# A four-layer kernel of 16 pipelined steps: the router's products one step later, beside the scores, and the queries' products between the halves of the last key unit

## The reference

```python
x = x + cross_attention(layernorm(x), ctx)      # Q = xWq+bq; K_hat = cos((ctx Wk+bk)Wr+br)
                                                # softmax(Q K_hat^T) @ (ctx Wv+bv)
x = x + sparse_attention(layernorm(x))          # top 8 earlier tokens by similarity, softmax over them,
                                                # message, gelu(mix*x + (1-mix)*msg, gain, bias) * scale
x = x + expert_mlp(layernorm(x))                # router: logits = xn @ Wr (8 experts), argmax,
                                                # p_max * (gelu(xn@W1[e]+b1[e]) @ W2[e] + b2[e])
```

## Time and profile before

| | us |
|---|---|
| median of 3 runs | 448.08 (447.14 to 448.7) |
| the profiled execution | 447.48 |
| its span, first to last instruction | 445.2 |
| PE busy | 409.2 (92%) |
| ACT busy | 257.2 (58%) |
| DVE busy | 248.7 (56%) |
| POOL busy | 236.4 (53%) |

### The profile page before, as it was taken

The page is one execution under the profiler, slowest core; times in us unless marked ns, Lnnn a source line. Parts: engine busy times, 40 slices in busy tenths (PEclk is TensorE's granted clock), DMA queues, the critical chain, the costliest instruction groups (busy, mean ns, idle before and its releaser), DMA issues.

```text
span 445.2 us, 10426 instructions
## 1 busy us (share of the span) xinstructions
PE 409.2 (92%) x3121; PEld 281.7 (63%) x3121; DVE 248.7 (56%) x808; ACT 257.2 (58%) x574; POOL 236.4 (53%) x458
## 2 busy tenths in 40 slices
PE   7858999999999999999994898699999999999991
PEld 6424454555545555455542677588999999998991
DVE  2637688788888989888984653534122212222210
ACT  0638778888988988889874646452333232424240
POOL 0733766767787887878855584642232322232210
PEclk9989999999999999999997999899999999999998
DMA  9988999797878979778965671454776656565100
GB/s 187 233 213 218 204 302 257 197 226 184 257 188 221 206 193 286 197 210 200 287 216 210 212 257 44 142 197 157 243 281 224 177 201 206 174 196 194 57 0 0
DMA packets 119449, 87.45 MB, mean 196 GB/s; under 512 B 78622, under 2 KB 109088, under 8 KB 119268
## 3 DMA queue, kind: packets, MB, share of 16 engines
q1 hardware_dynamic: 112820, 76.49, 61.1%
q0 software_dynamic: 3744, 9.46, 7.0%
q10 hardware_dynamic: 2832, 0.86, 1.1%
HBM read 79.15 MB, written 8.53 MB: 197 GB/s over the span
## 4 chain that ended last, share of the span: by engine, by line
PE 80%; issue 6%; POOL 4%; ACT 3%; DVE 3%; DMA 1%; SPq 1%; DVEq 0%; POOLq 0%; ACTq 0%
PE pK L1481 17%; PE pT L1468 17%; PE pT L1443 11%; PE pK L1443 11%; PE b L1389 5%; PE b L1626 4%; PE b L1522 4%; PE b L1586 3%; PE b L1565 3%; PE b L1615 2%; PE b L1549 1%; DMA XF<-in_ctx_dram 1%; PE pK L1389 1%; POOL f_row L408 1%; PE b L1634 1%
## 5 line engine op out<-in xcount | busy, mean ns | idle before, releaser
L1258 ACT ACTIVATE XF<-pT,b_now 128x128 f32<-128x128 f32 x184 | 52.6, 369 | 99.4 <-PE pT L1468 95.7
L1481 PE MATMUL pK<-W,XF 128*128 x368 | 86.2, 385 | 3.2 <-issue 2.1
L1468 PE MATMUL pT<-XF,stage 128*128 128x128 f32 x736 | 87.3, 275 | 0.7 <-issue 0.7
L1468 PEld LDWEIGHTS pT<-XF,stage 128*128 128x128 f32 x736 | 86.2, 192 | 2.4 <-issue 1.2
L1481 PEld LDWEIGHTS pK<-W,XF 128*128 128x128 f32 x368 | 68.4, 192 | 13.7 <-issue 5.3
L408 POOL DMA_INDIRECT f_row<-rows_by_token,token_i x23 | 23.5, 1021 | 90.3 <-DMA out_dram<-XF,token_i 67.7
L1443 PE MATMUL pK<-stage,Wkr 128*128 128x512 f32 x128 | 61.6, 605 | 0.5 <-DVE Wkr L721 0.5
L1443 PE MATMUL pT<-stage,Wkr 128*128 128x512 f32 x128 | 60.3, 593 | 1.6 <-DVE stage L717 1.6
L779 DVE TENSOR_TENSOR stage<-stage 128x512 f32<-128x512 f32 x64 | 46.2, 721 | 0.6
L1231 ACT ACTIVATE stage<-stage 128x512 f32<-128x512 f32 x64 | 40.5, 635 | 9.8 <-DVE stage L779 9.4
L717 DVE STREAM_TRANSPOSE stage<-XF 128x1024 f32<-128x1024 f32 x32 | 39.4, 1230 | 3.4 <-DMA XF<-in_ctx_dram 2.3
(11 more groups left out here) (192 smaller groups left out, 669.4 us busy)
## 6 DMA issues: line engine op xcount, KB each, us to landing
stage<-in_L_ffn_W_dram SPq DMA_DIRECT2D x23, 1024.0 KB, 6.0
stage<-in_ctx_dram SPq DMA_DIRECT2D x32, 512.0 KB, 5.1
XF<-in_ctx_dram SPq DMA_DIRECT2D x252, 64.0 KB, 2.6
W<-in_L_ffn_W_dram SPq DMA_DIRECT2D x8, 1024.0 KB, 7.2
rows_by_token<-rows_out SPq DMA_DIRECT2D x16, 256.5 KB
ctx_last<-in_ctx_dram SPq DMA_DIRECT2D x64, 32.0 KB, 4.5
X<-in_x_dram SPq DMA_DIRECT2D x1, 1536.0 KB, 7.3
tokens_by_expert<-no_token POOLq DMA_DIRECT2D x2, 576.0 KB, 4.5
```

Source lines behind the costliest of these rows:

```text
L1258: ins = act.activation(f_hT[b][:, n * P:(n + 1) * P], pT[i][:, (n % 4) * P:(n % 4 + 1) * P], ACT.Gelu, bias=b1_now[:, b, n:n + 1])
L1468: mm = pe.matmul(pT[i][:, (n % 4) * P:(n % 4 + 1) * P], W1[q][:, c, n * P:(n + 1) * P], f_inT[:, q % 2, c * P:(c + 1) * P], start=c == 0, ...
L1481: mm = pe.matmul(p_out, f_hT[q % 2][:, n * P:(n + 1) * P], W2[:, bass.ds(e, 1), n, :].rearrange("p o d -> p (o d)"), start=n == 0, stop=n ...
```

## The change

No instruction is added or dropped; the four edits are these.

1. PE: `router` leaves the end of the step, where it stood between `value_project` and the next step's first key unit. It is now issued one step later, between that first key unit and `scores`, for group `s-5`. The last one, `router(11)`, comes behind the loop. DVE's `logits_copy` follows it.
2. PE: the four products of `queries` are split in two pairs. Each pair stands behind one of the two 128x512 products of the last key unit: the new function `last_unit_and_queries` issues product `r` of the unit, then the two query products of half `r`. ACT's `queries` moves behind `turn(s, 3)`.
3. PE: `rank` moves behind `xn_T`; `h_T` and `probs_T` change places (and ACT's copies of them with them).
4. DVE and POOL: most of the step is in a new order.

```diff
@@ -476,34 +476,37 @@
             for s in range(1, NG):
                 if s >= 2:
                     rstd_h(s - 2)
+                last_key(s)
+                if s >= 2:
+                    normal_h(s - 2)
+                if s >= 6 and s % 2 == 0:
+                    count_pair(s // 2 - 3)
+                    tokens_of(s // 2 - 3)
+                if s >= 7 and s % 2:
+                    scatter(s // 2 - 3, (0,) if s + 1 < NG else (0, 1))
+                if s >= 2:
                     base(s - 2)
-                    normal_h(s - 2)
+                last_value(s - 1)
+                if s == NG - 1:
+                    gather(0)
+                if s + 1 < NG:
+                    rstd_x(s + 1)
+                if s + 1 < NG:
+                    normal_x(s + 1)
+                if s >= 4:
+                    rstd_out(s - 4)
                 if s == 3:
                     own_parts()
                 if s >= 3:
                     mix(s - 3)
-                last_key(s)
-                last_value(s - 1)
-                if s >= 2:
-                    messages(s - 2)
-                if s == NG - 1:
-                    gather(0)
-                if s >= 6:
-                    if s % 2 == 0:
-                        count_pair(s // 2 - 3)
-                        tokens_of(s // 2 - 3)
-                    else:
-                        scatter(s // 2 - 3, (0,) if s + 1 < NG else (0, 1))
-                if s >= 4:
-                    rstd_out(s - 4)
                 if s + 1 < NG:
-                    rstd_x(s + 1)
-                    normal_x(s + 1)
                     add_bv(s + 1)
                 if s in (2, 3):
                     no_tokens(s - 2)
                 if s >= 7 and s % 2 and s + 1 < NG:
                     scatter(s // 2 - 3, (1,))
+                if s >= 2:
+                    messages(s - 2)
 
             base(14)
             rstd_h(14)
@@ -1035,62 +1038,63 @@
             for s in range(1, NG):
                 if s >= 2:
                     residual_stats(s - 2)
-                if s + 1 < NG:
-                    next_stats(s + 1)
                 if s >= 2:
                     residual_moments(s - 2)
                 ctx_turned(s, 1)
+                if s >= 5:
+                    logits_copy(s - 5)
+                if s + 1 < NG:
+                    next_stats(s + 1)
+                if s + 1 < NG:
+                    next_moments(s + 1)
+                score_max(s - 1)
+                whole(s, 0)
+                if s >= 6 and s % 2 == 0:
+                    route(s // 2 - 3)
+                if s >= 7 and s % 2:
+                    places(s // 2 - 3)
+                    probability(s // 2 - 3)
+                inverse_sumA(s - 1)
+                fraction(s, 0)
                 if s >= 3:
                     inverse_sumB(s - 3)
-                    weights(s - 3)
-                score_max(s - 1)
-                if s >= 6:
-                    if s % 2 == 0:
-                        route(s // 2 - 3)
-                    else:
-                        places(s // 2 - 3)
-                        probability(s // 2 - 3)
-                if s + 1 < NG:
-                    next_moments(s + 1)
-                inverse_sumA(s - 1)
-                whole(s, 0)
                 if s + 1 < NG:
                     ctx_turned(s + 1, 0)
-                else:
+                if s == NG - 1:
                     plan_experts(1)
-                fraction(s, 0)
-                if s == 15:
                     plan_rows(1)
                 if s >= 4:
                     residual_out(s - 4)
+                if s >= 4:
                     out_stats(s - 4)
+                if s >= 4:
+                    out_moments(s - 4)
+                whole(s, 1)
+                if s >= 2:
+                    masked(s - 2)
+                fraction(s, 1)
+                if s >= 3:
+                    weights(s - 3)
+                if s >= 2:
+                    small_turned(s - 2)
+                if s >= 2:
+                    top(s - 2)
+                mean_value(s - 1)
+                if s >= 2:
+                    mark(s - 2)
+                if s >= 2:
+                    picks(s - 2)
+                whole(s, 2)
                 if s >= 3:
                     weights_T(s - 3)
                 if s >= 2:
-                    small_turned(s - 2)
-                if s >= 4:
-                    out_moments(s - 4)
-                if s >= 2:
-                    masked(s - 2)
-                whole(s, 1)
-                if s >= 2:
-                    top(s - 2)
-                fraction(s, 1)
-                if s >= 2:
-                    mark(s - 2)
-                whole(s, 2)
-                mean_value(s - 1)
-                if s >= 2:
-                    picks(s - 2)
                     select(s - 2)
+                whole(s, 3)
                 fraction(s, 2)
-                whole(s, 3)
                 fraction(s, 3)
                 if s >= 2:
                     selected_max(s - 2)
                 residual(s - 1)
-                if s >= 4:
-                    logits_copy(s - 4)
                 if s == 1:
                     scalars()
                 if s == 13:
...
@@ -1326,15 +1331,15 @@
                     scalars()
                 if s >= 4:
                     gelu_y(s - 4)
-                probsT_copy(s - 1)
                 if s >= 2:
                     hT_copy(s - 2)
+                probsT_copy(s - 1)
                 turn(s, 1)
                 sine(s, s % 2, 0)
                 turn(s, 2)
-                queries(s)
                 sine(s, s % 2, 1)
                 turn(s, 3)
+                queries(s)
                 oT_copy(s - 1)
                 if s >= 4:
                     xn3T_copy(s - 4)
@@ -1587,6 +1592,21 @@
                                        start=c == 0, stop=c == DC - 1)
                 mm.then_inc(S["qproj"], 1)
 
+            def last_unit_and_queries(g):
+
+                pe.wait_ge(S["ctxT_r"], 2 * g + 2)
+                at_least(pe, S["turns_r"], 4 * g)
+                pe.wait_ge(S["xnT_cp"], g + 1)
+                at_least(pe, S["hT_cp"], g - 1)
+                for r in range(DC):
+                    mm = pe.matmul(p_turns[3], Wkr[:, r, P:2 * P], ctx_T[1][:, r], start=r == 0, stop=r == DC - 1)
+                    if r == DC - 1:
+                        mm.then_inc(S["kproj"], 1)
+                    for c in range(DC):
+                        mm = pe.matmul(p_q[:, r * P:(r + 1) * P], Wq[:, c, r * P:(r + 1) * P], xnT[:, c, :],
+                                       start=c == 0, stop=c == DC - 1)
+                mm.then_inc(S["qproj"], 1)
+
             def value_T(g):
                 pe.wait_ge(S["o_r"], g + 1)
                 for c in range(DC):
@@ -1647,21 +1667,22 @@
 
             for s in range(1, NG):
                 ctx_project(s, 0, 0)
+                if s >= 5:
+                    router(s - 5)
                 scores(s - 1)
+                xn_T(s)
                 if s >= 7 and s % 2:
                     pe.wait_ge(S["logits_r"], s - 4)
                     rank(s // 2 - 3)
-                xn_T(s)
                 ctx_project(s, 0, 1)
-                probs_T(s - 1)
                 if s >= 2:
                     h_T(s - 2)
+                probs_T(s - 1)
                 ctx_project(s, 1, 0)
                 if s >= 2:
                     similar(s - 2)
                 values(s - 1, max(0, (s - 5) // 2))
-                queries(s)
-                ctx_project(s, 1, 1)
+                last_unit_and_queries(s)
                 if s >= 2:
                     small_scores(s - 2)
                 value_T(s - 1)
@@ -1670,12 +1691,11 @@
                 if s >= 3:
                     message(s - 3)
                 value_project(s - 1)
-                if s >= 4:
-                    router(s - 4)
                 if s == 1:
                     pe.wait_ge(S["b1_ld"], 16)
                     transposed(p_b1, b1_rows[:], "b1_tr")
 
+            router(11)
             in_T(*ring(0))
             scores(15)
             up(*ring(0), 0)
```

More of the change, by code:

```diff
@@ L1100, in _ @@
                     plan_used(0)
+            logits_copy(11)
             residual_stats(14)
```

## The result

| | before | changed |
|---|---|---|
| median of the runs | 448.3 (447.14 to 448.7, 4 runs) | 457.95 (456.51 to 460.15, 4 runs) |
| span of the profiled execution | 445.2 | 454.4 |
| PE busy | 409.2 | 411.1 |
| DVE busy | 248.7 | 258.7 |

The ratio is 1.022, with a 95% interval of 1.0171 to 1.0268: slower, where 446.2 was forecast. Some executions of any kernel here fall into a slower state of the chip: the medians hold all runs, the ratios leave those out. DVE carries 10 us more although no instruction was added.

A forecast was written before the change was run, and what follows sets the result against it. PE was taken to bound the loop. Against the profiled 447.48 us, +0.1 - 0.75 + 0.9 - 2.1 = -1.85 gave 445.6; with the median 0.6 above that execution, 446.2 us, range 441.3 to 450.6.

The forecast's parts named there:

- Steps 6 to 14: Loop steps 6 to 14: even and odd steps each lose 0.4 us and gain 0.31, +0.9 us over 9 steps.
- rival B: End of even steps: POOL and DVE's alternation feeds itself, up to 0.9 us a pair of steps, 450.9 us; chance 0.2.
- Odd steps: POOL in odd steps: `scatter` starts where `count_pair` does and takes as long; loss 0.4 us a step as in even ones.
- Blocking: POOL's stretch before `mixed`: one or two meetings with DVE of 0.3 to 0.5 us, `mixed` at 12.1 us into the step.
- The point of decision: PE's waits in the loop: a mean of about 0.6 us a step decides for rival B.
- The router: PE: `router` beside `scores` costs 0.13 us instead of 0.44, saving 0.31 a step, 3.4 us in all on PE.
- `rank` behind `xn_T`: PE: moving `rank` costs 0, since it stays within the array shape it had.
- The rival by which `router` pays the change of shape: PE: shape changes cost the same in any order, so `router` saves nothing; folded into a 448.2 us rival, chance 0.16.
- Queries: PE, last key unit: splitting the queries costs 0, bounds a gain or loss of 0.1 us a step.
- Step 15: POOL in step 15: both scatters ahead of `gather(0)`, inside its wait, bring `scores(15)` forward; -2.1 us, bounds -0.5 and -3.5.
- The 1.1 us given back: Step 15: `mix(12)` behind `rstd_out(11)`, 0.7 us, then `weights_T` and `select`, 0.4, come late and reduce 3.15 to 2.05.
- PE's clock: Step 15: less idle time keeps PE's clock up, some 0.2 us, against tokens up to 1 us late.

The follow-up runs named there:

- e7: Changed kernel with both sums of `messages` cut to 8 of 256 columns, order kept; 446.69 us, ratio 0.9954 to the kernel before.
- e8: e1 with `router` directly behind `scores` instead of ahead of it, and `logits_copy` behind `score_max`; 449.5 us, ratio 1.0048 to the kernel before.
- e10: Kernel before with step 15's scatters ahead of `gather(0)` and `router` one step later, ahead of `scores`; 444.69 us, ratio 0.9903.
- e4: Kernel before with only step 15's two scatters moved ahead of `gather(0)` on POOL; 444.99 us, ratio 0.9912.
- e1: Kernel before with the change's order on PE and ACT only, `logits_copy` one step later; 448.25 us, ratio 0.9991.
- e5: Kernel before with e1 and e4 together: new PE and ACT order, step 15's scatters ahead of `gather(0)`; 445.32 us, ratio 0.9929.
- e11: Changed kernel with `gather(0)` put back ahead of both scatters in step 15; 461.64 us, ratio 1.028 to the kernel before.
- e12: Kernel before with both sums of `messages` cut to 8 of 256 columns, as control for e7; 447.98 us, ratio 0.9979.
- e2: Kernel before with the change's order on POOL and DVE only, PE's and ACT's loops as before; 462.36 us, ratio 1.0308.

## Why the prediction was wrong

- **Steps 6 to 14, +0.9 forecast, +13.2 measured.** This is the step that failed. The mechanism, an alternation of POOL and DVE that feeds itself, was named as rival B, but its price was worked out as in the forecast. There `onehot` was placed by "so I put it at 4.9", counted from PE's step start as if DVE began its step there, and the lateness at the step's end was charged once, 0.25 and 0.15 us. In fact that lateness moves the start of the next `onehot`: `residual_stats` begins 1.72 us into the step (190.89 less 189.17; before 0.32, 153.87 less 153.55), `onehot` ends at 5.91 and `mixed` at 13.14, where 12.1 was forecast. POOL's stretch itself was nearly right, 7.23 for 6.8 plus 0.4 of blocking. A delay that returns to its own start does not add once, it sets the period: the parts of the path had to be summed and held against PE's 13.8 a step. The trace of the kernel before gave most of the sum: 6.8 and 0.4 on POOL, `weights_T` and `select` 0.4, a `whole` 0.4, two `fraction`s at 0.93, and DVE from `residual_stats` to `onehot` 4.4 (158.28 less 153.87) make 14.3. That is rough, since the 4.4 holds a wait of 0.44 for `scores`, and some 0.5 for `residual` is left out; but it stands over 13.8.
- **Odd steps.** "In odd steps `scatter` starts at the same point as `count_pair` and takes as long" was wrong by a microsecond: 8.22 to `mixed` against 7.23 (the first scatter takes 1.64 us, and the last operation of `rstd_x`, which starts with a `fraction`, 1.11 instead of 0.57).
- **Blocking.** "One or two such meetings of 0.3 to 0.5 us" were charged to the wrong side. Before, POOL's operations took the delay (L460 1,166 ns, `fraction` 696 in steps 7 to 14) and POOL had slack; now `fraction` takes one too (971, L460 1,065), and it is on the cycle. The prediction cited a lock on the port pair from the Trainium skill, page SBUF — State Buffer, section SBUF: two separate sides. e7 agrees (971 to 691 ns when most of the other side's work goes), and in odd steps a `fraction` that starts beside the scatter and ends between the two sums of `messages` takes 1.78 us. But "it makes no matter how small an instruction is" holds for the one that is held up (128x1 in `rstd_x`, 1.11 us), not for the one that holds the other: in e7 the sums of `messages` are as many as before, only shorter.
- **The point of decision.** Of B it says "It decides from a mean wait of about 0.6 us a step". PE's waits came to 1.1 to 1.3, so the sign of B was right; its price of 0.9 a pair of steps was 2.9. B's own time, 450.9, also lies outside the stated range, which ends at 450.6.
- **The router, 0.31 a step forecast.** 0.20 in even steps: the two changes of shape go, as forecast, but the 0.24 of its own stays 0.24. In e8, behind `scores`, it is 0.10: within one array shape the order counts, and the taken 0.13 is nearer to that of the other order. The reason was not tested. In odd steps `rank` behind `xn_T`, costed at 0, takes 0.09 more: with it the stretch from `scores` to the end of the next key unit grows by 0.135 in e10, by 0.045 before. That leaves 0.16 on average. The rival by which `router` pays the change of shape beside `scores` too is refuted for its two old neighbours, `value_project` and the key unit, which both got 0.1 us shorter.
- **Queries, 0: right.** Last key unit and queries take 2.805 us, 2.807 before.
- **Step 15, -2.1 forecast, -4.2 measured.** The mechanism is right, the two terms mis-sized. For the place -2.1 was taken; up to `out_T(11)` it is -2.8, and -3.4 in e4. The 1.1 us given back to `mix`, `weights_T` and `select` is not there: in the changed kernel `mixed` ends at 251.78, and `message` starts at 252.33, right behind `out_T`. For PE's clock "some 0.2" was taken, and up to 1 us of late tokens against it; behind `out_T(11)` the granted clock of 1.00 instead of 0.50 goes with -1.4, though PE waits 0.58 there for the last `sine`. In e4 the place alone left the clock at 0.50. What raised it in the changed kernel was not tried.
- **What cuts gains short.** e1, e4 and e5 brought `scores(15)` forward 2.9 to 4.1 us, and their tails are 1.7 to 2.9 us longer, with single waits of 0.5 to 1.2 us of PE on counts, tokens and expert rows. That the tail takes the gain back is not shown: e11, whose `scores(15)` comes 12 us late, has a tail of 201.17 us too, and each figure is from one execution. Up to 0.7 of the gain lies in the start and steps 1 to 3, which take 70.3 to 72.0 us in the profiles of all kernels here.

## What to carry to other kernels

When a reordering puts a step's late work of one engine in front of what another needs to begin the next step, write down the closed path through the engines, sum its parts over one period, and compare that with the bound engine's period; a sum of waits against a fixed step start misses it. The sign to look for is who waits for whom: while DVE waits for PE the blocking is free (e12), and once DVE waits for POOL it lengthens every step (e7). Move one thing at a time: here one moved pair of DMA issues was worth 0.9% by itself (e4), and together with the rest of POOL's and DVE's reordering the kernel lost 3.1% (e2).

## What the runs showed of the hardware

- Beside a group of the same array shape a router of 16 products of 8 columns costs 0.24 us ahead of it and 0.10 behind it (e5, e8).
- `rank`'s four small products add 0.045 us ahead of `xn_T` (before) and 0.135 behind it (e10); behind it the key unit that follows takes 1.800 instead of 1.719.
- `value_project` ahead of `router` in step 15 takes 1.06 us at a granted clock of 1.00 (changed kernel) and 2.01 at 0.50 (before), start to start.
- `STREAM_TRANSPOSE` of 128x1024 on DVE is not slowed by POOL: 30 of its 32 instances in the changed kernel have POOL work beside them for over 0.3 us, and the longest takes 1.25 us, the two alone 1.24. Of the 64 `fraction`s the 6 alone take 0.69 us, the 58 beside POOL work 0.92 in the mean and up to 1.79; a `whole` goes from 0.42 up to 0.72.
